# The carry of the running sums in the attention's edge pass: from VectorE to GpSimd

## The reference

```python
w_m = (efeat @ W_msg + b_msg).reshape(E, in_f, -1)
w_a = (efeat @ W_attn + b_attn).reshape(E, in_f, -1)
h_src = feat[src][:, :, None]
e1 = w_m * h_src
e2 = w_a * h_src
seg_max = jax.ops.segment_max(e2, dst, num_segments=N)
ex = jnp.exp(e2 - seg_max[dst])
denom = jax.ops.segment_sum(ex, dst, num_segments=N)
ft = jax.ops.segment_sum(e1 * (ex / denom[dst]), dst, num_segments=N)
return ft.sum(axis=1)
```

## Time and profile before

| | |
|---|---|
| Median of 3 runs | 3127.6 us (3121.86 to 3134.39) |
| The profiled execution (span) | 3126.8 us |
| PE / DVE / ACT / POOL busy | 75% / 71% / 54% / 45% of the span |
| Edge pass, about 1387 us to 3013 us | 44 blocks, about 35 us each from the third on |
| DVE busy from 1480 to 2940 us | 1374.5 of 1460 us |
| Granted clock of TensorE, same stretch | 0.82 of full speed |
| GpSimd busy, same stretch | 1051.5 of 1460 us, all of it gathers |

### The profile page before, as it was taken

One profiled execution on the slowest core, in us unless ns is written; L12 is line 12 of the kernel. 1 busy time (PEld: TensorE's weight loads), 2 busy tenths in 40 slices (PEclk: granted clock), 3 DMA queues, 4 the chain that ended last, 5 costly groups with the idle time before them and its releaser, 6 DMA issues. The chain is left out here.

```text
span 3126.8 us, 38694 instructions
## 1 busy us (share of the span) xinstructions
PE 2351.3 (75%) x8098; PEld 1032.6 (33%) x8099; DVE 2224.5 (71%) x3656; ACT 1698.7 (54%) x6693; POOL 1398.1 (45%) x1220
## 2 busy tenths in 40 slices
PE   1888887656675998854788888888888888888840
PEld 1444443232453555331232223322232222322220
DVE  7999993110233554113999999999999999999967
ACT  0777770000011111105888888888888888888800
POOL 3000000676323000015767776777777776777303
PEclk9999997768676999875888888888788878888875
DMA  1000000333125444200222222222222222222213
GB/s 17 0 0 0 0 0 6 85 87 88 52 62 171 150 149 146 73 19 17 64 67 72 63 80 67 63 72 76 70 65 72 63 80 67 63 72 68 70 47 89
DMA packets 122372, 201.38 MB, mean 64 GB/s; under 512 B 55271, under 2 KB 76664, under 8 KB 116448
## 3 DMA queue, kind: packets, MB, share of 16 engines
q1 hardware_dynamic: 84320, 170.52, 15.6%
q0 software_dynamic: 38016, 30.45, 6.2%
HBM read 72.73 MB, written 128.17 MB: 64 GB/s over the span
## 5 line engine op out<-in xcount | busy, mean ns | idle before, releaser
L1481 POOL DMA_INDIRECT hs<-h_table,gix x880 | 1103.8, 1254 | 451.2 <-issue 271.5
L1574 ACT ACTIVATE e<-wps,hs 128x32 f32<-128x32 f32 x5632 | 1029.8, 402 | 235.2 <-PE wps L1505 142.3
L1505 PE MATMUL wps<-w_edge,ef 18*128 18x512 f32 x1760 | 577.6, 707 | 316.1 <-ACT e L1574 135.1
L1527 PE MATMUL slot_sums<-e,ident 128*128 128x512 f32 x1408 | 761.3, 691 | 9.7 <-DVE e L1676 7.0
L1527 PEld LDWEIGHTS slot_sums<-e,ident 128*128 128x128 f32 x1408 | 296.6, 222 | 493.3 <-issue 464.3
L1505 PEld LDWEIGHTS wps<-w_edge,ef 18*128 18x128 f32 x1760 | 159.1, 200 | 691.5 <-ACT e L1574 274.8
L358 PE MATMUL acc<-q_hot,lo_hot 128*128 128x400 bf16 x1200 | 306.0, 337 | 48.7 <-DVE q_hot L337 46.8
L1611 DVE TENSOR_TENSOR e<-wps,hs 128x2048 f32<-128x2048 f32 x132 | 301.9, 2287 | 41.1 <-PE wps L1505 34.0
L375 ACT CAST edges<-acc 128x400 f32 x600 | 293.5, 492 | 59.0 <-PE acc L362 32.5
L337 DVE TENSOR_SCALAR q_hot<-qcol,qT 128x400 bf16<-128x400 bf16 x1200 | 293.9, 322 | 9.7 <-PE acc L362 9.5
L456 POOL DMA_INDIRECT got<-in_edge_rows,ix x224 | 224.9, 1004 | 100.7 <-issue 92.7
(11 more groups left out here) (322 smaller groups left out, 2104.3 us busy)
## 6 DMA issues: line engine op xcount, KB each, us to landing
rows_state<-states SPq DMA_DIRECT2D x44, 1280.0 KB
rows_shift<-shifts SPq DMA_DIRECT2D x44, 640.0 KB
edges_order<-got SPq DMA_DIRECT2D x56, 256.0 KB
got_order<-edges_order SPq DMA_DIRECT2D x56, 256.0 KB, 2.9
ef_order<-efT SPq DMA_DIRECT2D x56, 256.0 KB, 3.0
hs<-h_table,gix POOLq DMA_INDIRECT x880
ef<-ef_order SPq DMA_DIRECT2D x44, 320.0 KB, 2.9
msg<-m_parts SPq DMA_DIRECT2D x10, 480.0 KB, 4.9
```

Source lines behind the costliest of these rows:

```text
L1481: nc.gpsimd.indirect_dma_start(out=hs[u][:, s, :], out_offset=None, in_=d["h_table"], in_offset=bass.IndirectOffsetOnAxis(ap=gix[u][:, s:s ...
L1505: nc.tensor.matmul(wps[:, bank, :], ef[u][k:k + KM, g * P:(g + 1) * P], w[k:k + KM, :], start=True, stop=True).then_inc(a_mult, 1)
L1527: ins = nc.tensor.matmul(sums[:, g % 2, :], ident[:, :], e[u][:, g * SLOTS + c, :], start=(c == 0), stop=(c == SLOTS - 1))
L1574: ins = nc.scalar.mul(e[u][:, s, at], wps[:, bank, at], hs[u][:, s, f:f + 1])
```

## The change

The carry is no longer issued by DVE but by POOL, once for each block, behind the 20 gathers that POOL issues for the block two later. POOL's instruction has the same operands, and the same waits, and one for `a_exp`, as ACT writes `scale`. It counts up a new semaphore, `a_carried`, on which DVE's `accumulate` of step 0 now waits. DVE's three calls of `carry` go: the one in `block_step` (40 times from the loop, 3 outside of it) and the one for the last block. POOL's last two are issued after its loop.

```diff
@@ POOL
                         gather(u, k * 2 + (u + 2), k + 2)
+                        carry(u, k * 2 + u, k * 16 + 16)
+
+                def carry(u, b, stored):
+
+                    pool.wait_ge(a_acc, b * BG + BG)
+                    pool.wait_ge(a_exp, b * (BG + 1) + 1)
+                    pool.wait_ge(a_stored[u], stored)
+                    nc.gpsimd.tensor_tensor(
+                        four(states[u][:, 0, :]), four(states[1 - u][:, BG - 1, :]),
+                        bc(scale[u][:, :].rearrange("p (i o) -> p i o", o=F), 2, 2), ALU.mult).then_inc(a_carried, 1)
 
                 gather(0, 0, 1)
                 gather(1, 1, 1)
                 turn(0)
                 with pool.Fori(1, BLOCKS // 2 - 1) as k:
                     turn(k)
+                carry(0, BLOCKS - 2, 16 * (BLOCKS // 2))
+                carry(1, BLOCKS - 1, 16 * (BLOCKS // 2))
@@ DVE
-                def carry(v, u, b, stored):
-
-                    dve.wait_ge(a_acc, b * BG + BG)
-                    dve.wait_ge(a_stored[u], stored)
-                    v.add(nc.vector.tensor_tensor(
-                        four(states[u][:, 0, :]), four(states[1 - u][:, BG - 1, :]),
-                        bc(scale[u][:, :].rearrange("p (i o) -> p i o", o=F), 2, 2), ALU.mult))
-
                 def accumulate(v, u, b, g):
@@
                     if g == 0:
+                        dve.wait_ge(a_carried, b + 1)
                         ins = nc.vector.tensor_tensor(states[u][:, 0, :], states[u][:, 0, :], total, ALU.add)
@@ block_step
                     shifted = up(v, u, 3)
-                    carry(v, w, b - 1, i * 16 + 16 * u)
                     v.wait(shifted)
                     shifted = up(v, u, 4)
@@ behind the loop
                 weigh(v, 1, BLOCKS - 1)
-                carry(v, 1, BLOCKS - 1, 16 * (BLOCKS // 2))
                 v.wait(v.n)
```

More of the change, by code:

```diff
@@ L1401, in attention_edges @@
         sums = ctx.enter_context(nc.psum_tensor("slot_sums", [P, 2, 2 * CH], F32))
-        a_w, a_mult, a_read_v, a_read_s, a_sub, a_exp, a_weighed, a_sum, a_halved, a_acc, a_shift, a_last, a_step, a_go = (
-            sem("a_" + s) for s in "w mult read_v read_s sub exp weighed sum halved acc shift last step go".split())
+        a_w, a_mult, a_read_v, a_read_s, a_sub, a_exp, a_weighed, a_sum, a_halved, a_acc, a_shift, a_last, a_step, a_go, a_carried = (
+            sem("a_" + s) for s in "w mult read_v read_s sub exp weighed sum halved acc shift last step go carried".split())
         a_gix = [sem("a_gix0"), sem("a_gix1")]
```

## The result

The changed kernel takes 3146.3 us in the median of 4 runs (3144.93 to 3151.37), the kernel before beside it 3126.5: a ratio of 1.0063 [1.0047, 1.0080]. It is slower, by 20 us where no change was forecast. The profiled execution has a span of 3144.4 us.

What follows compares the result with a forecast made beforehand. It took PE's sums, ACT's slots, exponentials and slots again as the bounding cycle, with DVE having time to spare. 3126.8 - 1 + 0 to 1 gave 3126 to 3127, median 3127 us; range 3117 to 3146.

Steps and rivals of the forecast that it cites:

- DVE's removed instruction is worth nothing: Before L1711 on DVE: the 0.60 us saved a block become longer waiting for PE; about 1 us gained in all.
- DVE held by POOL, H = 1.05, absorbed: DVE standing for POOL's whole carry, H us a block, loses nothing at 1.05; blocks lose only from 1.10.
- in this trace POOL yields and DVE loses nothing: DVE's instructions keep their lengths beside POOL's gathers, five L1676 taking 5.76 us; so the carry's cost to DVE is 0.
- 26 us less DVE busy: Carry removed from DVE: 43 block steps at 0.60 us each lower its busy time by 26 us.
- The signs: Expected profile after: wait at L1711 about 60 us in all, unchanged blocks, POOL's carries about 1.05 us, gathers released by ACT.
- blocks of 35.2 us as before: Expected in the profile after: the length of a block stays at 35.2 us.
- three signs named for a wrong prediction: L1711's wait not growing with DVE's lengths unchanged; both DVE waits shrinking to nothing; gathers' start released by POOL itself.
- POOL's own waits are over by then: When POOL's last gather ends at 2054.22, the carry's inputs are ready, so its waits cost POOL nothing.
- the ring: The cycle taken to set the pace: PE's sums, ACT's slots 5 and 6 or DVE's subtractions, ACT's exponentials and slots.
- Rival 4, the clock: Moved DVE times change which matmuls run slow on PE; 0.3 us a block either way, 13 us; chance 0.03.
- PE's own times are not moved where the forecast holds: Reason for giving the clock shift little chance: PE's instruction times stay unchanged if the forecast is right.
- 17, 12 and 12 blocks: 41 blocks grouped by DVE's idle time before the second L1631 and L1711, read as time to spare; 1.45 us on average.

Runs made afterwards that it cites:

- e3: The kernel before with DVE's carry multiply removed and done by nobody, its waits kept; 0.9996 of before.
- e8: The kernel before, with POOL waiting behind its gathers as for the carry and counting up a semaphore, for which nobody waits; 1.0053 of before.
- g3: The kernel before, with POOL's two waits and count behind the gathers done twice, on chip 15, where ACT has pauses; 1.0051 of before.
- f3: The kernel before, with POOL's two waits and count behind the gathers done twice, on chip 3; 0.9997 of before.
- e6: The kernel before, DVE's carry kept, plus POOL's waits and a fill of an unused tile behind the gathers, DVE waiting for it early; 1.0036 of before.
- f1 to f4: Chip 3: before plus POOL's count alone, waits and count ahead of next gathers, or both twice; changed kernel with carry ahead of next gathers; 0.9997 to 1.0009.
- e2: The kernel before, with DVE's own carry counting up `a_carried` and the first sum waiting for it, POOL unchanged; 0.9998 of before.
- g1: The kernel before, with POOL only counting up one semaphore behind a block's gathers, on chip 15; 1.0005 of before.

## Why the prediction was wrong

- **DVE's removed instruction is worth nothing**: right. e3 gives 0.9996.
- **DVE held by POOL, H = 1.05, absorbed**: right in size (1.0) and in effect, by luck in part. The instruction takes 1.26 us at its shortest, where I had 1.05 and, from the page "GPSIMD Engine Reference" of the Trainium skill, section "Performance versus the Vector engine", an estimate of 1.1 to 1.2; but its median is 2.03, as DVE holds it too. That "in this trace POOL yields and DVE loses nothing" did not carry over from gathers to the carry: DVE lost 1.0 us a block. (The gather does read SBUF, its indices `gix`; and 0.6 + 0.43 is 1.03, not 1.05, which changes nothing.) The forecast of 26 us less DVE busy fell with it (39 blocks x 1.0 came back).
- **The signs**: the wait before L1716 came out at 56.9 where about 60 were forecast. That is luck: the 60 went with blocks of 35.2 us and no hold, and 39 us of hold and blocks 0.53 us longer met it from both sides, while the wait before the second L1631 fell from 20.1 to 5.1. L1676 and L1633 have grown as was said for a hold, and the next gathers are released by ACT. The sign that failed is "blocks of 35.2 us as before": they are 35.69. None of the three signs named for a wrong prediction came, as none looked at ACT or at POOL's sequencer.
- **The step that failed**: "POOL's own waits are over by then". I took as the time at which POOL meets the waits the end of its last gather, 2054.22. The engine is there then; its sequencer was there at 6 us behind the first sum, near 2034, and in the changed kernel is held until the last sum, ahead of 2045.36. The wait is about 11 us long, and the pair of waits alone costs the whole loss (e8, 1.0053). Behind it are queued not only the next gathers, which have the time, but the loop's branch, and that is the one thing I never named. The branch of 2069.1 beside gathers until 2088.8 stands in the trace of before and would have told where the sequencer is. That the branch is what does the harm is argued, not shown.
- **The term left out**: ACT's pauses. I read "0.37 <-issue" in the earlier trace rows and took ACT's work in its slots as a constant. They are 0.67 us a block in the ring before and grew by 0.23; PE's sum of step 1 (+0.19 us) grew with them.
- **Rival 4, the clock**, named what over half of the loss goes with, and its size (0.3 us a block, 13 us, against the 13 us estimated above), with a chance of 0.03 because "PE's own times are not moved where the forecast holds". They were moved, by a way outside of DVE. The prediction had the clock's three kinds of block in hand: its 17, 12 and 12 blocks with 0.64 to 1.04, 1.32 to 1.44 and 2.2 to 2.4 us of idle time are, one for one, the blocks of 34.6, 35.1 and 36.0 us. It took them as spare time of DVE and did not ask what would move a block from one kind to another. The range ended at 3146 and the chance of slower was 0.12; most of both went to a hold that costs nothing.

## What to carry to other kernels

A wait given to an engine is met by its sequencer, far ahead of the work that stands in its queue: take the time at which it is reached from the sequencer's own rows (branches, register instructions), and name everything that is queued behind it there, loop branches too. Idle time under "issue" in the ring that sets the pace is a term of the sum like any other and can be lengthened by an engine that shares no data with it. Look at the lengths of single blocks beside the granted clock: where they fall into kinds, a small delay can cost more than itself by moving blocks from one kind to the next. Time a change of half a per cent on more than one chip: the same kernel took 1.0051 of before on chip 15 (g3) and 0.9997 on chip 3 (f3).

## What the runs showed of the hardware

- A multiply of a 128x512 f32 tile by a 128x256 one, each number used twice, takes POOL 1.26 us at the shortest and 2.03 in the median behind the gathers, beside DVE; DVE loses 1.0 us a block to it. A fill of 128x512 takes 0.55 us (e6) and costs DVE nothing.
- A gather takes 1.87 and 1.92 us in the median beside DVE's subtractions and multiplies of 128x1024 with both inputs in SBUF (L1658, L1676, kernel before), and 0.94 beside L1611, which reads PSUM, and beside L1640.
- POOL's sequencer is twelve gathers, 19.7 us, ahead of its engine where it takes its loop's branch in the kernel before.
- With a granted clock of 0.85 a block of the kernel before takes 34.6 us, with 0.81 35.1 or 36.0; in f1 to f4 on chip 3 it takes 34.1 with either.
- ACT stood still for 0.56 to 0.67 us in a run of 80 short instructions in each block on four chips where POOL had no added wait (e3, e2, g1, before), and not on a fifth, on which before takes 3010.6 us against 3070.0 to 3122.2 on the others.
